# A graph network's attention layers: the destinations' term spread by products with a repeated column, and the softmax chain one group earlier

## The chip, the cores and the metric

The kernel runs on one core of one Trainium2 chip. The metric is the device time of one execution in microseconds (us); lower is better.

## The reference, cut to what matters

Two residual blocks stand behind each other: two graph-convolution layers, then five attention layers over the same 50,000 edges, sorted by destination, and 3,125 nodes. Only the attention layers are touched by the change. Each of them computes, for two heads (H = 2) of 128 features (D = 128):

```python
xw = x @ W
xj = xw[src].reshape(-1, H, D) + edge_emb.reshape(-1, H, D)
xi = xw[dst].reshape(-1, H, D)
alpha = jnp.einsum('ehd,hd->eh', xi, att_i) + jnp.einsum('ehd,hd->eh', xj, att_j)
alpha = jax.nn.leaky_relu(alpha, NEG_SLOPE)
amax = jax.ops.segment_max(alpha, dst, num_segments=N)
ea = jnp.exp(alpha - amax[dst])
denom = jax.ops.segment_sum(ea, dst, num_segments=N)
alpha = ea / (denom[dst] + EPS)
msg = xj * alpha[..., None]
aggr = jax.ops.segment_sum(msg, dst, num_segments=N)
return aggr.mean(axis=1) + b
```

Every node also has an edge to itself. The first einsum is the destinations' attention term: one number for each node and head, `x @ (W att_i)`.

## The kernel before

**Tiles.** The nodes are 25 tiles of 128 (NT = 25). The edges are 391 tiles of 128 (REAL), cut into 15 chunks: thirteen of 28 tiles, one of 16, one of 11. A chunk is worked off in groups of four tiles (seven groups in a chunk of 28).

**Gathers.** The node rows with their source term stand in `table` in HBM. GpSimd (POOL) issues one indirect DMA for each edge tile, `ring<-table,srci`, line 502, into a ring of 60 slots. Gather t reuses the slot of tile t - 60, so from the 61st on it first waits for the semaphore `sums` of the group that held this tile. POOL is thus at most 60 tiles ahead of TensorE.

**Destinations' term.** It has to lie in `ai_rows` as one row of 3,200 numbers for each head, the same in all 128 partitions. Before, VectorE (DVE) makes it by 50 dot products per layer (line 1079, into `node_ai`), TensorE (PE) transposes them (line 774), ScalarE (ACT) copies them out, and SyncE (SP) writes them to HBM and reads them back to all partitions (line 431, two transfers of 1600 KB). From `ai_rows` ACT then copies for each edge tile a window of 24 columns for both heads to `ai_win` (line 567, `windows(layer, c)`, 28 copies for a chunk), whose start it loads into a register.

**Old rows.** TensorE also transposes the 25 tiles of the layer's input (line 765, `old_tile`), and ACT copies each out of PSUM (line 587), for the products with W of the self edges (`self_tile`, line 782).

**Softmax chain.** For every chunk there is a chain of small steps between DVE, TensorE and ACT, with four names on DVE and TensorE alike: `chain_alpha` (add the gathered source term, leaky relu, transpose), `chain_scan` on DVE (running maxima), `chain_rows` (maxima across the tiles), `chain_cols` (final maxima and differences) followed by ACT's exponentials (`exps`, lines 573 and 575), and `chain_probs` (transpose back, write `est`). The chain of chunk c + 1 is woven into the groups of chunk c: `chain_alpha` stands at group number `lag(c)`, the next steps at the two groups behind it, `chain_probs` behind the last group. Group by group, DVE makes `pw` (`weigh`, line 1165), TensorE forms the sums (`aggregate`, lines 750 and 752), and DVE adds them to `acc` (`add_group`, line 1201).

**Order on ACT at a layer's start.** The copies of the old rows, then `windows(layer, 0)`, `windows(layer, 1)`, and only then `exps(layer, 0)`. `windows(layer, 1)` waits until DVE has used the windows of chunk 0.

**Order around it.** There is no scheduler: all queues are written out by hand, and semaphores tie them.

## Time and profile before

| what | value |
|---|---|
| time, median of 3 runs | 4135.25 us (4131.62 to 4136.99) |
| the profiled execution, its own time | 4165.07 us |
| its span in the profile | 4163.3 us |
| mean granted TensorE clock | 0.57 of full speed |
| busy: PE, DVE, ACT, POOL | 65%, 47%, 17%, 52% |
| DMA, mean over the span | 51 GB/s |

The profile shows one execution. A busy share is an average over the convolution part (the first 500 us) and five attention layers of some 720 to 750 us each. No engine is near 100%; what counts is which wait ends last, and that is read from the waits and from the order of time, not from the shares. "remote" and "issue" as releasers mean that the profile names no instruction that the engine waited for.

### The profile page before, as it was taken

The page shows a single profiled execution, that of the slowest core. Times are in us where ns is not written, and L with a number is a line of the kernel's source. Part 1 is how long each engine was busy: PE and PEld are TensorE (multiplying, and loading weights), DVE is VectorE, ACT ScalarE, POOL GpSimd, SP SyncE. Part 2 cuts the span into 40 slices and gives each one's busy share as a digit, 9 for nine tenths or more (in the row PEclk, how much of TensorE's full clock was granted, in tenths as well). Part 3 has the DMA queues.
Part 4 walks back from the last instruction along what each step waited for, and adds up shares of the span by engine and source line. Part 5 has one row for each costly group of instructions (what it writes and reads, how often), then busy time and mean ns, then how long its engine had stood idle before and what let it go on. Part 6 is the DMA issues. An engine that isn't in the chain of part 4 may idle for free.

```text
span 4163.3 us, 50211 instructions
## 1 busy us (share of the span) xinstructions
PE 2692.6 (65%) x14802; PEld 2154.4 (52%) x14802; DVE 1972.1 (47%) x6923; ACT 723.6 (17%) x3237; POOL 2146.3 (52%) x2359
## 2 busy tenths in 40 slices
PE   7778426665791666669266666917666691766668
PEld 6678425554561555546155555615555460555556
DVE  9866624444452444444344444534444452444445
ACT  0077321111121111101211111121111121111111
POOL 0066366666415665650656656165656615665661
PEclk9955555555575555556555555855555585555558
DMA  3211122222102222210212222022222102222221
GB/s 113 90 46 49 51 78 50 50 48 54 38 18 78 49 48 49 53 43 11 83 47 48 47 55 46 18 80 49 49 48 54 44 19 79 49 48 48 48 46 32
DMA packets 114664, 213.66 MB, mean 51 GB/s; under 512 B 35266, under 2 KB 76518, under 8 KB 113110
## 3 DMA queue, kind: packets, MB, share of 16 engines
q0 software_dynamic: 62560, 130.25, 13.8%
q1 hardware_dynamic: 51830, 80.19, 5.9%
q8 instruction: 119, 1.95, 0.2%
q14 instruction: 155, 1.27, 0.1%
HBM read 198.50 MB, written 11.80 MB: 51 GB/s over the span
## 4 chain that ended last, share of the span: by engine, by line
PE 23%; DVE 21%; POOL 19%; issue 17%; another core or an unknown queue 12%; DVEq 2%; ACTq 2%; ACT 2%; DMA 1%; POOLq 0%; SPq 0%
POOL ring L502 19%; PE bank L750 8%; PE bank L752 4%; DVE acc L1201 4%; PE bank L758 3%; DVE prod L1079 2%; PE bank L695 2%; ACTq L567 2%; DVE ring L870 1%; DVE ai_win L1098 1%; DVE alpha L1101 1%; DVEq L1024 1%; PE bank L820 1%; DVE ai_rows L955 1%
## 5 line engine op out<-in xcount | busy, mean ns | idle before, releaser
L502 POOL DMA_INDIRECT ring<-table,srci x1955 | 1877.1, 960 | 1225.5 <-issue 533.3
L750 PE MATMUL bank<-pw,ring 128*128 128x48 f32 x3910 | 1205.6, 406 | 110.3 <-DMA ring<-table,srci 61.0
L1201 DVE TENSOR_TENSOR acc<-acc,bank 128x72 f32 x1955 | 449.9, 230 | 1398.3 <-remote 745.9
L750 PEld LDWEIGHTS bank<-pw,ring 128*128 128x128 f32 x3910 | 950.0, 297 | 265.2 <-issue 132.6
L567 ACT COPY ai_win<-ai_rows 128x48 f32 x1955 | 349.5, 229 | 1496.5 <-issue 1165.6
L752 PE MATMUL bank<-onehot,est 128*36 128x24 f32 x3910 | 601.5, 240 | 0.0
L752 PEld LDWEIGHTS bank<-onehot,est 128*36 128x36 f32 x3910 | 369.3, 144 | 168.3
L708 PE MATMUL bank<-identf,alpha 128*56 128x128 f32 (+2 forms) x75 | 29.1, 388 | 472.9 <-DVE alpha L1117 259.6
L509 POOL TENSOR_TENSOR S<-S 128x128 f32<-128x128 f32 x125 | 57.2, 458 | 466.1 <-ACT S L579 461.6
L708 PEld LDWEIGHTS bank<-identf,alpha 128*56 128x56 f32 (+2 forms) x75 | 8.9, 119 | 484.8 <-issue 261.8
L484 POOL TENSOR_TENSOR ring<-ring,acc 128x512 f32<-128x512 f32 x98 | 115.2, 1177 | 277.6 <-ACT ring L532 273.8
L1098 DVE TENSOR_TENSOR ai_win<-ai_win,onehot 128x1344 f32<-128x1344 f32 (+2 forms) x75 | 109.2, 1456 | 276.9 <-issue 231.3
L758 PE MATMUL bank<-onehot,identf 128*128 128x504 f32 x310 | 208.9, 787 | 0.0
L721 PE MATMUL bank<-ones,cin 1*56 1x1 f32 (+1 forms) x300 | 37.2, 224 | 252.6 <-DVE cin L1148 161.4
L695 PE MATMUL bank<-onehot,ring 128*128 128x24 f32 x784 | 172.4, 387 | 38.8 <-DVE acc L1050 30.1
L695 PEld LDWEIGHTS bank<-onehot,ring 128*128 128x128 f32 x784 | 169.5, 331 | 40.5 <-issue 28.3
L573 ACT ACTIVATE phi<-phi 1x2 f32<-1x2 f32 x75 | 15.2, 203 | 941.0 <-issue 587.3
L734 PE MATMUL bank<-identf,bwd 56*128 56x56 f32 (+2 forms) x75 | 25.5, 340 | 227.4 <-ACT bwd L575 193.7
L721 PEld LDWEIGHTS bank<-ones,cin 1*56 1x56 f32 (+1 forms) x300 | 30.8, 185 | 273.4 <-DVE cin L1148 168.4
L1165 DVE TENSOR_TENSOR pw<-onehot,est 128x192 f32<-128x192 f32 x490 | 166.8, 353 | 0.5 <-issue 0.5
L782 PE MATMUL bank<-Wl,S 128*128 128x256 f32 x250 | 152.8, 715 | 0.0
L734 PEld LDWEIGHTS bank<-identf,bwd 56*128 56x128 f32 (+2 forms) x75 | 13.1, 175 | 250.7 <-ACT bwd L575 212.9
(205 smaller groups left out, 3278.1 us busy)
## 6 DMA issues: line engine op xcount, KB each, us to landing
ring<-table,srci POOLq DMA_INDIRECT x1955
ai_rows<-lo_dram SPq DMA_DIRECT2D x28, 896.0 KB, 4.3
ai_rows<-ai_dram SPq DMA_DIRECT2D x10, 1600.0 KB
at<-in_attr SPq DMA_DIRECT2D x65, 224.0 KB
table<-ring SPq DMA_DIRECT2D x25, 325.0 KB, 3.4
x_mid<-ring SPq DMA_DIRECT2D x1, 1600.0 KB, 7.0
result<-ring SPq DMA_DIRECT2D x24, 64.0 KB
vrow<-v_dram SPq DMA_DIRECT2D x20, 64.0 KB
```

The costliest lines, as they stand in the source:

```text
L484: GP.tensor_tensor(z, z, b1s.unsqueeze(1).broadcast_to((P, GRP, D)), ALU.add).then_inc(pre_add, 1)
L502: nc.gpsimd.indirect_dma_start(out=ring[:, slot(t), :], out_offset=None, in_=table, in_offset=bass.IndirectOffsetOnAxis(ap=srci[:, t:t + 1 ...
L567: ins = nc.scalar.copy(ai_win[:, t - TC[c] + k, :, :], ai_rows[:, :, bass.ds(base[k], WIN)])
L695: ins = nc.tensor.matmul(grp_sum(g, k)[:, 0:WIN], rows[:, g % 3, k, :], onehot[:, t, :], start=True, stop=True)
L750: nc.tensor.matmul(o[:, 0:H * WIN], ring[:, slot(t), 0:D], pw[:, g % 3, k, :, :].rearrange("p h w -> p (h w)"), start=True, stop=True)
L752: ins = nc.tensor.matmul(o[0:EC, H * WIN:REG * WIN], est[:, c % 2, t - TC[c], :], onehot[:, t, :], start=True, stop=True)
L758: nc.tensor.matmul(bank[3][:, 0:21 * WIN], identf[:, :], onehot[:, 0:21, :].rearrange("p t w -> p (t w)"), start=True, stop=True)
L782: nc.tensor.matmul(bank[3][:, 0:H * D], S[:, j, D:2 * D], Wl[:, layer % 2, :], start=True, stop=True).then_inc(s_ps, 1)
L1079: V.tensor_tensor_reduce(out=dump[:, d % NDUMP, :], in0=xt[:, j, 0:D], in1=vrow[:, 2 * h + i, :], scale=1.0, scalar=v17[:, layer, h, FA:FA ...
L1098: link(V.tensor_tensor(win, win, onehot[:, ts, :].unsqueeze(2).broadcast_to((P, k, H, WIN)), ALU.mult))
L1165: V.tensor_tensor(pw[:, g % 3, 0:n, :, :], onehot[:, t:t + n, :].unsqueeze(2).broadcast_to((P, n, H, WIN)), est[:, c % 2, k:k + n, HF:HF + ...
L1201: V.tensor_tensor(win, win, grp_sum(g, k).rearrange("p (r w) -> p r w", r=REG), ALU.add)\
```

## The change

- The destinations' term: TensorE multiplies the transposed old rows by a weight block whose 128 columns are all the same vector W att_i (`V4[...].broadcast_to((P, P))`). Each product gives the term of 512 nodes in all 128 partitions at once, so `ai_rows` is filled by copies out of PSUM: head 0 by ACT, head 1 by DVE, seven each. The 50 dots, the transpose, the write to HBM and the two broadcast reads go.
- The old rows are transposed four at a time into one PSUM bank and copied out by seven ACT copies of 512 columns instead of 25 of 128.
- For the self edges the term comes out of `self_tile`, whose product gets two more columns; DVE copies them to `node_ai` for each of the 25 tiles.
- `lag(c)` is the number of groups less 4 instead of less 3: the four chain steps move one group earlier, on DVE and on TensorE.

```diff
-DOTS = 2 * H * NT
+DOTS = H * NT
+TQ = 4
+NQ = -(-NT // TQ)
 def lag(c):
-    return max(0, len(GC[c]) - 3)
+    return max(0, len(GC[c]) - 4)
...
             for layer in range(LAYERS):
                 table_tiles(layer)
-                sp.wait_ge(aiT_sb, layer + 1)
-                sp.dma_start(ai_dram, aiT).then_inc(aiT_w, 16)
-                sp.wait_ge(aiT_w, 16 * (layer + 1))
-                for h in range(H):
-                    sp.dma_start(ai_rows[:, h, :], ai_flat[:, h * NP:(h + 1) * NP].broadcast_to((P, NP)))\
-                        .then_inc(ai_in, 16)
...
+        def ai_copy(copy, engine, layer, q, h):
+            a, b = q * TQ * P, min(NP, (q + 1) * TQ * P)
+            engine.wait_ge(ai_ps, H * NQ * layer + H * q + h + 1)
+            copy(ai_rows[:, h, a:b], bank[4 + h][:, 0:b - a]).then_inc(ai_sb[h], 1)
...
-                for j in range(NT):
-                    act.wait_ge(tr_ps, n + j + 1)
-                    nc.scalar.copy(S[:, j, D:2 * D], bank[6 + j % 2][:, 0:P]).then_inc(tr_sb, 1)
-                    if j == 1:
-                        act.wait_ge(aiT_ps, layer + 1)
-                        nc.scalar.copy(aiT, bank[3][0:H * NT, 0:P]).then_inc(aiT_sb, 1)
-                act.wait_ge(ai_in, 16 * H * (layer + 1))
+                def old_rows(q):
+                    j0, j1 = q * TQ, min(NT, q * TQ + TQ)
+                    act.wait_ge(tr_ps, n + j1)
+                    nc.scalar.copy(S[:, j0:j1, D:2 * D],
+                                   bank[6 + q % 2][:, 0:(j1 - j0) * P].rearrange("p (j n) -> p j n", n=P)).then_inc(tr_sb, 1)
+
+                for q in range(NQ):
+                    old_rows(q)
+                    if q:
+                        ai_copy(nc.scalar.copy, act, layer, q - 1, 0)
+                ai_copy(nc.scalar.copy, act, layer, NQ - 1, 0)
+                for h in range(H):
+                    act.wait_ge(ai_sb[h], NQ * (layer + 1))
                 windows(layer, 0)
                 windows(layer, 1)
                 exps(layer, 0)
...
+            def ai_product(layer, q):
+                j0, j1 = q * TQ, min(NT, q * TQ + TQ)
+                pe.wait_ge(tr_sb, NQ * layer + q + 1)
+                for h in range(H):
+                    if q:
+                        pe.wait_ge(ai_sb[h], NQ * layer + q)
+                    nc.tensor.matmul(bank[4 + h][:, 0:(j1 - j0) * P].rearrange("p (j n) -> p j n", n=P),
+                                     V4[:, layer, 2 * h:2 * h + 1].broadcast_to((P, P)), S[:, j0:j1, D:2 * D],
+                                     start=True, stop=True).then_inc(ai_ps, 1)
...
-                for j in range(NT):
-                    for h in range(H):
-                        dot(layer, j, h, 0, node_ai[:, h, j:j + 1])
...
                 def self_rows(j):
                     v.wait_ge(s_ps, n + j + 1)
+                    V.tensor_copy(node_ai[:, :, j], bank[3][:, H * D:H * D + H])
                     V.tensor_tensor(S[:, j, :], bank[3][:, 0:H * D], ebl[:, :], ALU.add)\
                         .then_inc(s_sb, 1)

+                for q in range(NQ):
+                    ai_copy(V.tensor_copy, v, layer, q, 1)
```

The first place is TensorE's queue at the start of the second attention layer, behind the last products of the layer before. L765 are the transposes of the old rows, L774 that of the dots, L708 is `chain_alpha` of chunk 0; the words in brackets are the semaphores waited for. Before:

```order
L765 MATMUL bank<-identf,ring 128x128 [waits h_sb,lay_w]
L765 MATMUL bank<-identf,ring 128x128 [waits h_sb]
L774 MATMUL bank<-identf,node_ai 50x128 [waits dotted]
L765 MATMUL bank<-identf,ring 128x128 [waits tr_sb,h_sb] x23
L708 MATMUL bank<-identf,alpha 56x128 [waits al_ready,tr_sb,aiT_sb]
```

Now (L772 the transposes, L780 the products with the repeated column):

```order
L772 MATMUL bank<-identf,ring 128x128 [waits h_sb] x8
L780 MATMUL bank<-S,V 128x512 [waits tr_sb]
L780 MATMUL bank<-S,V 128x512
L772 MATMUL bank<-identf,ring 128x128 [waits h_sb,tr_sb]
L772 MATMUL bank<-identf,ring 128x128 [waits h_sb] x3
L780 MATMUL bank<-S,V 128x512 [waits ai_sb0,tr_sb]
L780 MATMUL bank<-S,V 128x512 [waits ai_sb1]
```

Nothing waits for `dotted` any more, and each pair of products stands behind four transposes and waits for a copy of ACT and for the two copies of the pair before.

The second place is TensorE's queue at the end of a chunk of 28 tiles, between its last group and the first group of the next chunk. L721, L725 and L727 are `chain_cols`, L734 and L735 `chain_probs`. Before, behind the last group:

```order
L752 MATMUL bank<-onehot,est 36x24
L721 MATMUL bank<-ones,cin 56x1 [waits scan2]
L721 MATMUL bank<-ones,cin 56x1
L725 MATMUL bank<-phi,ones 128x2 [waits exp_phi]
L727 MATMUL bank<-phi,sel 128x1 x2
L734 MATMUL bank<-identf,bwd 128x56 [waits exp_al]
L735 MATMUL bank<-identf,fwd 128x56
L750 MATMUL bank<-pw,ring 128x48 [waits gath1,est_ready,added,issued,p_ready]
```

Now (the same steps are L725, L729, L731, L738 and L739, a group is L754 and L756):

```order
L725 MATMUL bank<-ones,cin 56x1 [waits scan2]
L725 MATMUL bank<-ones,cin 56x1
L729 MATMUL bank<-phi,ones 128x2 [waits exp_phi]
L731 MATMUL bank<-phi,sel 128x1 x2
L754 MATMUL bank<-pw,ring 128x48 [waits added,p_ready]
```

`chain_cols` has moved ahead of the last group; behind that group only `chain_probs` is left.

## Rows read from the trace of the kernel before

**Rows 1.** The page, costliest groups: the gathers (busy, mean ns, idle before).

```profile
L502 POOL DMA_INDIRECT ring<-table,srci x1955 | 1877.1, 960 | 1225.5 <-issue 533.3
```

**Rows 2.** Instructions of line 502: what POOL waited for (us, times).

```profile
  PE bank L752: 358.1, 78
  remote: 285.6, 124
```

**Rows 3.** Order of time, POOL: first gather, second and fourth attention layer (start, us).

```profile
1252.18 0.98 POOL L502 DMA_INDIRECT ring<-table,srci  x1 [5.21 <-DMA table<-ring]
...
2720.94 0.96 POOL L502 DMA_INDIRECT ring<-table,srci  x1 [5.51 <-DMA table<-ring]
```

**Rows 4.** Order of time, POOL: the 61st gather of each of the five layers.

```profile
607.94 0.94 POOL L502 DMA_INDIRECT ring<-table,srci  x1 [17.46 <-PE bank L752]
1348.45 0.94 POOL L502 DMA_INDIRECT ring<-table,srci  x1 [21.54 <-PE bank L752]
2094.80 0.94 POOL L502 DMA_INDIRECT ring<-table,srci  x1 [19.25 <-PE bank L752]
2814.84 0.94 POOL L502 DMA_INDIRECT ring<-table,srci  x1 [17.49 <-PE bank L752]
3540.53 0.94 POOL L502 DMA_INDIRECT ring<-table,srci  x1 [21.03 <-PE bank L752]
```

**Rows 5.** Order of time, ACT: first window copies, second and fourth attention layer.

```profile
1296.37 1.48 ACT L567 COPY ai_win<-ai_rows 128x48 f32 x8 [0.21 <-issue]
...
2744.31 1.77 ACT L567 COPY ai_win<-ai_rows 128x48 f32 x10 [0.21 <-issue]
```

**Rows 6.** Order of time, ACT: later window copies of the same two layers.

```profile
1317.59 0.23 ACT L567 COPY ai_win<-ai_rows 128x48 f32 x1 [2.57 <-issue]
1318.99 0.23 ACT L567 COPY ai_win<-ai_rows 128x48 f32 x1 [1.17 <-issue]
...
1336.94 4.13 ACT L567 COPY ai_win<-ai_rows 128x48 f32 x24 [0.20 <-issue]
...
2805.51 1.95 ACT L567 COPY ai_win<-ai_rows 128x48 f32 x11 [0.47 <-issue]
```

**Rows 7.** Order of time, second attention layer: ACT's last relu, TensorE, the broadcasts.

```profile
1247.58 0.31 ACT L610 ACTIVATE ring<-y 128x128 f32<-128x128 f32 x1 [0.75 <-DVE y L1298]
...
1259.61 0.41 PE L774 MATMUL bank<-identf,node_ai 128*50 128x128 f32 x1 [15.46 <-DVE node_ai L1079]
...
1261.74 0.81 SPq L431 DMA_DIRECT2D ai_rows<-ai_dram  x2
```

**Rows 8.** Order of time, all engines, from one chunk's last group through the next chunk.

```profile
1427.43 1.32 DVE L1201 TENSOR_TENSOR acc<-acc,bank 128x72 f32 x4 [0.46 <-remote]
1427.57 0.94 POOL L502 DMA_INDIRECT ring<-table,srci  x1 [2.77 <-remote]
...
1430.04 0.28 DVE L1160 TENSOR_TENSOR bwd<-bank,fwd 56x128 f32<-56x128 f32 x1
...
1431.22 0.22 DVE L1174 COPY est<-bank 128x56 f32<-128x56 f32 x1 [0.90 <-PE bank L735]
...
1432.47 0.62 DVE L1165 TENSOR_TENSOR pw<-onehot,est 128x192 f32<-128x192 f32 x2
...
1432.88 0.66 PE L750 MATMUL bank<-pw,ring 128*128 128x48 f32 x2 [1.70 <-DMA ring<-table,srci]
...
1436.58 0.94 POOL L502 DMA_INDIRECT ring<-table,srci  x1 [4.32 <-PE bank L752]
...
1456.49 0.41 PE L708 MATMUL bank<-identf,alpha 128*56 128x128 f32 x1 [5.04 <-issue]
...
1480.82 0.94 POOL L502 DMA_INDIRECT ring<-table,srci  x1 [4.32 <-PE bank L752]
```

**Rows 9.** Groups of instructions by form, PE: 504-column filler products, old-row transposes.

```profile
L758 PE MATMUL bank<-onehot,identf 128*128 128x504 f32 x310 | 208.9, 787 | 0.0
...
L765 PE MATMUL bank<-identf,ring 128*128 128x128 f32 x125 | 44.5, 427 | 78.0 <-issue 53.5 <-ACT S L587 14.0 <-ACT ring L554 10.4
```

More of the change, by code:

```diff
@@ L138, in program @@
         biasl = sb("biasl", [P, D])
-        vrow = sb("vrow", [P, 4, D])
+        vrow = sb("vrow", [P, H, D])
         V4 = sb("V4", [P, LAYERS, 4])
@@ L339, in program @@
         dotted = sem("dotted")
-        aiT_ps = sem("aiT_ps")
-        aiT_sb = sem("aiT_sb")
-        aiT_w = sem("aiT_w")
-        ai_in = sem("ai_in")
+        aj_read = sem("aj_read")
+        ai_ps = sem("ai_ps")
+        ai_sb = [sem(f"ai_sb{h}") for h in range(H)]
+        wv_sb = sem("wv_sb")
         tr_ps = sem("tr_ps")
@@ L391, in node_weights @@
             def node_weights(layer):
-                sp.dma_start(Wl[:, layer % 2, :], weights[layer * P:(layer + 1) * P, :]).then_inc(lay_w, 16)
+                sp.dma_start(Wl[:, layer % 2, 0:H * D], weights[layer * P:(layer + 1) * P, :]).then_inc(lay_w, 16)
                 sp.dma_start(ebl[:, :], edge_b[layer:layer + 1, :].broadcast_to((P, H * D))).then_inc(lay_w, 16)
                 sp.dma_start(biasl[:, :], biases[layer:layer + 1, :].broadcast_to((P, D))).then_inc(lay_w, 16)
-                for q in range(4):
-                    sp.dma_start(vrow[:, q, :], v_dram[4 * layer + q:4 * layer + q + 1, :].broadcast_to((P, D)))\
-                        .then_inc(lay_w, 16)
+                for h in range(H):
+                    q = 4 * layer + 2 * h + 1
+                    sp.dma_start(vrow[:, h, :], v_dram[q:q + 1, :].broadcast_to((P, D))).then_inc(lay_w, 16)
             def edge_weights(layer):
@@ L947, in _, with weight_columns @@
             v.sem_inc(V4_sb, 1)
+            def weight_columns(layer):
+                V.tensor_copy(Wl[:, layer % 2, H * D:H * D + H], V4[:, layer, 0:4:2]).then_inc(wv_sb, 1)
+            weight_columns(0)
             def pick(n, out):
@@ L1069, in _, with dot @@
             v.sem_inc(ln_coef, 1)
-            v.wait_ge(lay_w, 16 * 7)
+            v.wait_ge(lay_w, 16 * 5)
             dots = [0]
-            def dot(layer, j, h, i, out_col):
+            def dot(layer, j, h, out_col):
                 d = dots[0]
@@ L1078, in dot @@
                     v.wait_ge(dotted, d - NDUMP + 1)
-                V.tensor_tensor_reduce(out=dump[:, d % NDUMP, :], in0=xt[:, j, 0:D], in1=vrow[:, 2 * h + i, :], scale=1.0,
-                                              scalar=v17[:, layer, h, FA:FA + 1] if i else 0.0,
+                V.tensor_tensor_reduce(out=dump[:, d % NDUMP, :], in0=xt[:, j, 0:D], in1=vrow[:, h, :], scale=1.0,
+                                              scalar=v17[:, layer, h, FA:FA + 1],
                                               op0=ALU.mult, op1=ALU.add, accum_out=out_col).then_inc(dotted, 1)
@@ L1209, in _ @@
                 link(V.tensor_copy(node_aj[:, :, :], xt[:, :, D:ROW].rearrange("p j h -> p h j")))
-                for j in range(NT):
-                    for h in range(H):
-                        dot(layer, j, h, 0, node_ai[:, h, j:j + 1])
+                v.sem_inc(aj_read, 1)
                 link(V.tensor_tensor(ebl[:, :].rearrange("p (h f) -> p h f", h=H),
@@ L1252, in _ @@
                     if c == 10:
+                        if not final:
+                            weight_columns(layer + 1)
                         v.wait_ge(lay_e, 32 * (layer + 1))
@@ L1284, in _ @@
                 else:
-                    v.wait_ge(lay_w, 16 * 7 * (layer + 2))
+                    v.wait_ge(lay_w, 16 * 5 * (layer + 2))
                 for j in range(NT):
```

51 lines of the change are left out of this document (26 added, 25 removed).

## The prediction, made blind

> **What bounds the kernel now.** I read the costliest groups first, then what the gathers waited for, then the order of time at a layer's start and inside a layer. The gathers are the largest group, 1,877 us busy, yet POOL is idle for 1,225 us before them [rows 1]. Of that, 533 us are the 0.30 us between two gathers [rows 1]; 358 us are waits for TensorE's group sums and 286 us waits with no named releaser [rows 2], which in the order of time also fall on gathers that need a group's sums. So inside a layer POOL runs as far ahead as the ring of 60 slots lets it, then stands until a group is summed: a layer goes at the pace at which the first sums of each chunk come out, not at POOL's own 1.25 us for a gather.
>
> Two places hold these waits. The first is the 61st gather of each layer: stalls of 17.46, 21.54, 19.25, 17.49 and 21.03 us, 97 us together [rows 4]. The reader is to see that chunk 0 has not given its first sums when the ring is full. The second repeats at each chunk boundary: 4.32 us at 1436.58 [rows 8]. It comes again at 1480.82, 44.2 us later, as 4.32 us. There are eleven boundaries per layer, 55 in all, from the 89th gather to the 369th; most show about 4.3 us.
>
> **The start of a layer.** In the second attention layer ACT is free at 1247.9 [rows 7]. TensorE then waits 15.46 us for the dots, transposes them at 1259.61, the broadcasts go out at 1261.74, and ACT's first window copy starts at 1296.37 [rows 5, 7], 44.2 us after the first gather [rows 3]. What held it was not the broadcast alone: the 25 old-row copies stand ahead of it on ACT.
>
> Now the change. Dots, transpose, write and broadcasts go. TensorE can do two batches of transposes before ACT is free, then alternates: two products and four transposes per round. A 512-column product is not in the trace; the nearest is the filler of 504 columns, 208.9 us for 155 products (each shows as two rows), 1.35 us at the mix of clocks there; a transpose costs 44.5/125 = 0.36 us [rows 9]. A round is 2 x 1.35 + 4 x 0.36 = 4.1 us. Six rounds from 1248.5, a short seventh and the last copy end near 1274, 22 us after the first gather. ACT's and DVE's copies lie beside the products. So the windows start 22 us earlier than before in this layer.
>
> What is that worth? The trace has the answer without the change, because layers differ. In the fourth layer the windows already started 23.4 us after the first gather, in the second 44.2 us [rows 3, 5]. Yet the stalls are 17.49 and 21.54 us [rows 4]: 20.8 us earlier bought 4.05 us. The reason is ACT's pace. While POOL gathers, a window copy starts every 1.40 us and every fourth takes 2.80, 7.0 us for four; after POOL has stopped, 24 copies take 4.13 us [rows 6]. In the fourth layer the quick pace came back only at 2805.51 [rows 6], some 8 us after the gathers had stopped (2814.84 - 17.49 = 2797.4 [rows 4]). Chunk 0's exponentials stand behind the windows of chunk 1 on ACT, 56 copies in all, so at 7.0 us for four they cannot be through before the ring is full. What ends last is this return of the quick pace, and that hangs on POOL. With 0.195 us of stall per us of window start, 22 us gives 17.2 us of stall in each layer: 0.3 + 4.3 + 2.0 + 0.3 + 3.8 = **11 us** saved over five layers. The lower bound is 0; the upper one the whole 97 us [rows 4], if the slow pace does not come.
>
> At full TensorE clock the rounds would be shorter and the windows start up to 10 us earlier; by the same slope this is 2 us per layer at most. The Trainium skill (TensorE: Matmul & The Clock Gate, Part 1: The HAM clock gate) says that TensorE keeps its full clock of 2.4 GHz only while it is kept busy, and the products would keep it busier here. Its effect stays within those 2 us.
>
> The first gather itself waits for the table write [rows 3], whose dots stay. It does not move.
>
> **The chain one group earlier.** Take the boundary in rows 8. POOL gets the slots of the last group at 1427.57, issues four gathers (5.0 us) and stands 4.32 us until the next chunk's first group is summed, 9.01 us after 1427.57. In these 9 us DVE adds the last group (1427.43 to 1428.75), only then does the columns step (to 1430.32), ACT the exponential, TensorE the transposes, DVE `est` (1431.22) and `pw` (1432.47), TensorE the group (1432.88), POOL goes on at 1436.58. With the new order the columns step stands before the last group is added, and its exponential runs beside that addition. Then from 1428.75: `est` 1.25 us (1431.22 to 1432.47), 0.41 us to the group, 3.70 us to POOL: 1434.1 instead of 1436.58, **2.4 us** per boundary. The stall shrinks from 4.32 to 1.9, so it is not used up and all of 2.4 us would be on the path: 55 x 2.4 = 132 us.
>
> I don't take all of it. TensorE stands 5.04 us before `chain_alpha` [rows 8], and its fifth group was already through by then. Now it stands before the rows step for the scan instead, which DVE ends about 1 us later, and the sixth group follows. POOL's other stalls (2.8 us before 1427.57) release what the sums of the middle groups hold up, and a shorter stall at the boundary may lengthen them. Bounds: 0 and 2.4 us. I take two thirds, 1.6 us, since the chain in rows 8 is a strict sequence that the new order really shortens: 55 x 1.6 = **88 us**.
>
> **What it adds.** One more filler product per layer in the twelfth chunk, 1.35 us [rows 9], so 5 x 1.35 = 7 us if nothing hides it; I take 4. The 25 copies of two columns to `node_ai` in each layer lie in DVE's idle time (47% busy over the span); uncovered, at about the 0.2 us of a small copy (`est`, 0.22 us [rows 8]), 25 us in all. The seven pairs of products and their copies are in the 22 us above. Two vrow loads less and the moved wait for weights cost nothing: the loads go out in mid-layer.
>
> **Sum.** -11 - 88 + 4 = -95 us. The profiled execution took 4165.07 us (its span 4163.3), so one of after should show about 4070. It stands 30 us over the median of the runs, and I take the saving off both alike: 4135.25 - 95 = 4040 us.
>
> **The rivals.**
> - *Likeliest (0.45)*: both terms as above, 1.0 to 2.4 us per boundary: 3995 to 4085, 4040 in the middle.
> - *The chain gives nothing (0.22)*. POOL's stalls may be needed by the rest: ACT's pace of 7.0 us for four copies ends only when POOL stands [rows 6], and DVE sees sums late while POOL runs ("remote", 286 us [rows 2]). Then a shorter stall at the boundary comes back as a longer one two groups on, and the 9 us of stall in a chunk stay. For it: the waits without a releaser. Against: in rows 8 each step follows its cause within 0.5 us. Time: 4135 - 11 + 4 = 4128, to 4110 with a little of the chain's gain.
> - *The slow pace does not come at a layer's start (0.15)*. The 3.2 MB of broadcasts fall just where ACT turns slow. If they are its cause, 56 copies take some 10 us, chunk 0 is summed before the ring is full, and the 97 us of rows 4 go whole: 4135 - 97 = 4038 without the chain's gain, 3950 with it. Against: the slow pace lasts until POOL stops, long after the transfers. The Trainium skill (Runtime: NRT & Kernel Launch, Instruction fetch mechanics) says that an engine's instructions are fetched ahead and the fetch is mostly hidden; by it the 1.40 us per copy are not a lack of instructions, and ACT would do its windows at the quick pace once whatever loads the core is gone.
> - *Slower (0.10)*. TensorE's sixth group now stands behind the rows step and so behind DVE's scan. POOL needs its sums for the last four gathers of the chunk after next. If they come so late that POOL stands once more per chunk, a stall like the 2.77 us in rows 8 is added at each boundary and eats the 2.4: from +0 to 55 x 2.77 = 152 us, 4135 to 4287, I say 4175. It decides when the sixth group's sums come over 1.9 us later than now.
> - *No change to be told (0.08)*: the small terms cancel, 4127 to 4143. Under 0.2% (8.3 us) a measurement of this kernel can't be told from no change.
>
> **How the numbers follow.** The time is that of the likeliest, 4040. The range 3960 to 4127 takes the likeliest (0.45), nearly all of the second case (0.21) and most of the third (0.13), 0.79 together; the likeliest alone is 3995 to 4085. Faster: 0.45 + 0.21 + 0.15 = 0.81; within 0.2%: 0.08 and what the second case leaves, 0.09; slower: 0.10.
>
> **What the profile of after would show.** Right: window copies start 12 to 25 us after the first gather in every layer; the 61st gather's stall is near 17 us in all five; the boundary stall falls from 4.3 to about 2 us, and the distance of two boundary stalls from 44 to 42 or 42.5 us. Wrong, in order: a 61st gather without a stall (third case); boundary stalls shorter but 44 us apart (second); a new stall per chunk before the sixth group's slots (fourth). The weakest step is the two thirds of 2.4 us.

## The result, and the profile after

| | kernel before | changed kernel |
|---|---|---|
| median of the runs, us | 4136.12 (4 runs, 4131.62 to 4146.59) | 3939.68 (4 runs, 3930.15 to 3949.26) |
| ratio | | 0.9522, 95% interval 0.9488 to 0.9555 |
| profiled execution, us (its span) | 4165.07 (4163.3) | 3949.26 (3947.2) |

The change saves 196 us. The forecast was 95, and 3940 lies below its range (3960 to 4127). The direction was right and the size was half of it.

The table holds for one kind of chip. The experiments ran on five numbered chips, and these fall into two kinds: on two of them (9 and 4) the kernel before takes 4135 and 4132 us, as here, and on three (6, 11 and 12) it takes 3445 to 3448 us. On the one of these three where the changed kernel itself was run (6) it is 0.8% *slower*. I come to that below. "The first kind" are the chips at 4135 us, "the second kind" those at 3445.

Where the time went can be read from one group. These are the gathers of the changed kernel on the page (columns as in [rows 1]; its line 495 is line 502 of before):

```profile
L495 POOL DMA_INDIRECT ring<-table,srci x1955 | 1891.2, 967 | 1023.2 <-issue 536.8 <-remote 299.8 <-PE bank L756 139.3
```

The pauses between two gathers ("issue") and the gathers themselves are what they were [rows 1]. The two waits for group sums were 358.1 and 285.6 us [rows 2], together 643.7; now they are 139.3 and 299.8, together 439.1. That is 205 us less. Gathers and pauses took 18 us more. The two spans differ by 216 us; the 29 us that are left lie behind the last gathers of the layers. There the first two layers take 40 us less, for in before TensorE had a low clock in just these two (below), and the other three 12 us more.

The first place, the start of a layer. Order of time of the changed kernel, POOL, the 61st gather of each of the five layers, as in [rows 4]:

```profile
599.09 0.94 POOL L495 DMA_INDIRECT ring<-table,srci  x1 [10.39 <-PE bank L756]
...
1282.25 0.94 POOL L495 DMA_INDIRECT ring<-table,srci  x1 [12.60 <-PE bank L756]
...
1974.95 0.94 POOL L495 DMA_INDIRECT ring<-table,srci  x1 [16.52 <-PE bank L756]
...
2660.27 0.95 POOL L495 DMA_INDIRECT ring<-table,srci  x1 [16.49 <-PE bank L756]
...
3351.04 0.94 POOL L495 DMA_INDIRECT ring<-table,srci  x1 [16.50 <-PE bank L756]
```

Together 72.5 us instead of 96.8 [rows 4]: 24 us less, where 11 were forecast. TensorE and ACT in the second attention layer, in order of time: the products that spread the term, and the window copies that answer to [rows 5, 6]:

```profile
1195.86 1.88 PE L780 MATMUL bank<-S,V 128*128 128x512 f32 x4
1197.58 0.60 PE L772 MATMUL bank<-identf,ring 128*128 128x128 f32 x4
1198.02 1.88 PE L780 MATMUL bank<-S,V 128*128 128x512 f32 x4
```

```profile
1206.06 2.23 ACT L565 COPY ai_win<-ai_rows 128x48 f32 x12 [1.47 <-issue]
...
1217.91 0.23 ACT L565 COPY ai_win<-ai_rows 128x48 f32 x1 [1.87 <-issue]
1219.31 0.23 ACT L565 COPY ai_win<-ai_rows 128x48 f32 x1 [1.17 <-issue]
...
1251.51 0.23 ACT L565 COPY ai_win<-ai_rows 128x48 f32 x1 [2.57 <-issue]
1252.91 0.23 ACT L565 COPY ai_win<-ai_rows 128x48 f32 x1 [1.17 <-issue]
1254.31 0.23 ACT L565 COPY ai_win<-ai_rows 128x48 f32 x1 [1.17 <-issue]
1255.71 0.23 ACT L565 COPY ai_win<-ai_rows 128x48 f32 x1 [1.17 <-issue]
```

A round of two products and four transposes takes 2.16 us (1195.86 to 1198.02) and not 4.1, since TensorE had its 2.4 GHz here (granted clock 1.00 from 1195 to 1199 us). The windows start 12.6 us after the layer's first gather (at 1193.4), not 22; over the five layers it is 10.0 to 16.1 us. Then ACT falls into the slow pace of [rows 6] all the same: 1.40 us for a copy and 2.80 for every fourth. The first 12 copies still go at the quick pace, though POOL has been gathering for 12.6 us by then; I come back to that at the end. No broadcast runs any more. So the third rival, that the broadcasts cause the slow pace, is refuted.

The second place, the chunk boundary. Order of time of the changed kernel over one boundary, all engines, as in [rows 8]:

```profile
1477.46 0.15 DVE L1176 COPY carry_col<-bank 56x2 f32<-56x2 f32 x1 [1.75 <-remote]
...
1479.16 0.31 ACT L573 ACTIVATE bwd<-bwd 56x128 f32<-56x128 f32 x1 [9.19 <-issue]
1479.52 0.35 PE L738 MATMUL bank<-identf,bwd 56*128 56x56 f32 x1 [2.86 <-issue]
...
1481.27 1.31 DVE L1221 TENSOR_TENSOR acc<-acc,bank 128x72 f32 x4 [2.14 <-remote]
1481.40 0.94 POOL L495 DMA_INDIRECT ring<-table,srci  x1 [2.58 <-remote]
1482.50 0.21 DVE L1194 COPY est<-bank 128x56 f32<-128x56 f32 x1
...
1483.74 0.62 DVE L1185 TENSOR_TENSOR pw<-onehot,est 128x192 f32<-128x192 f32 x2
...
1484.15 0.66 PE L754 MATMUL bank<-pw,ring 128*128 128x48 f32 x2 [4.17 <-DVE pw L1185]
...
1487.85 0.94 POOL L495 DMA_INDIRECT ring<-table,srci  x1 [1.47 <-PE bank L756]
```

The columns step, the exponential and its transposes are through before the last group is added, and `est` follows the addition at once. From the slots of the last group to POOL's next start it is 6.45 us (1481.40 to 1487.85) where it was 9.01. The stall is 1.47 us instead of 4.32. The boundary before this one in the same trace is at 1446.42 and the next at 1529.17, so they lie 41.4 us apart, where it was 44.2. This boundary is a fair sample: in POOL's order of time the 55 stalls at the boundaries are 235.6 us before and 92.5 now (4.28 and 1.68 us each), and the mean distance of two boundaries goes from 44.0 to 41.1 us. All other waits behind the 88th gathers of the layers go from 285.8 to 251.5 us together.

### The profile page after: what moved, and what is told of

Read it like the earlier page. It is cut to its first block, busy times and chain, and to the rows that moved or that the text cites. A ratio compares the mean times of both kernels' runs of the same rounds, so it can differ in the third digit from the quotient of the medians.

```text
span 3947.2 us, 50027 instructions
## 1 busy us (share of the span) xinstructions
PE 2719.3 (69%) x14947; PEld 2152.7 (55%) x14947; DVE 1939.4 (49%) x6588; ACT 738.0 (19%) x3177; POOL 2160.9 (55%) x2359
## 4 chain that ended last, share of the span: by engine, by line
DVE 35%; PE 21%; another core or an unknown queue 18%; issue 13%; DVEq 5%; ACTq 4%; POOL 3%; ACT 2%; DMA 0%; POOLq 0%; SPq 0%
DVE acc L1221 9%; PE bank L754 6%; PE bank L762 4%; ACTq L565 3%; PE bank L756 3%; POOL ring L495 2%; DVE pw L1185 2%; DVEq L1044 2%; DVE ai_win L1118 2%; PE bank L699 2%; DVE alpha L1121 2%; DVEq L1221 2%; DVE ee L1120 1%; DVE prod L1099 1%
## 5 line engine op out<-in xcount | busy, mean ns | idle before, releaser
L754 PE MATMUL bank<-pw,ring 128*128 128x48 f32 x3910 | 1206.7, 406 | 247.5 <-DVE pw L1185 180.5
L754 PEld LDWEIGHTS bank<-pw,ring 128*128 128x128 f32 x3910 | 935.8, 295 | 382.3 <-DVE pw L1185 190.8
L1221 DVE TENSOR_TENSOR acc<-acc,bank 128x72 f32 x1955 | 449.9, 230 | 1247.8 <-remote 726.8
L565 ACT COPY ai_win<-ai_rows 128x48 f32 x1955 | 358.4, 229 | 1860.7 <-issue 1749.9
L756 PE MATMUL bank<-onehot,est 128*36 128x24 f32 x3910 | 600.2, 239 | 7.8 <-issue 7.8
L756 PEld LDWEIGHTS bank<-onehot,est 128*36 128x36 f32 x3910 | 368.6, 144 | 179.6 <-issue 12.6
L717 PE MATMUL bank<-identf,fwd 56*1 56x56 f32 (+1 forms) x150 | 24.3, 259 | 262.3 <-issue 132.6
L729 PE MATMUL bank<-phi,ones 1*128 1x2 f32 x150 | 41.5, 344 | 174.5 <-ACT phi L571 174.4
L797 PE MATMUL bank<-Wl,S 128*128 128x258 f32 x250 | 153.7, 716 | 0.0
L541 ACT ACTIVATE ring<-ring,acc 128x128 f32<-128x128 f32 x392 | 124.4, 388 | 56.9 <-PE bank L699 42.3
L729 PEld LDWEIGHTS bank<-phi,ones 1*128 1x128 f32 x150 | 35.0, 289 | 176.6 <-ACT phi L571 175.0
```

What stands on the lines that cost most here:

```text
L541: ins = nc.scalar.activation(rows[:, g % 3, k, :], pre[:, g % 3, k, :], ACT.Relu, scale=n_e[:, t:t + 1])
L565: ins = nc.scalar.copy(ai_win[:, t - TC[c] + k, :, :], ai_rows[:, :, bass.ds(base[k], WIN)])
L754: nc.tensor.matmul(o[:, 0:H * WIN], ring[:, slot(t), 0:D], pw[:, g % 3, k, :, :].rearrange("p h w -> p (h w)"), start=True, stop=True)
L756: ins = nc.tensor.matmul(o[0:EC, H * WIN:REG * WIN], est[:, c % 2, t - TC[c], :], onehot[:, t, :], start=True, stop=True)
L797: nc.tensor.matmul(bank[3][:, 0:H * D + H], S[:, j, D:2 * D], Wl[:, layer % 2, :], start=True, stop=True).then_inc(s_ps, 1)
L1221: V.tensor_tensor(win, win, grp_sum(g, k).rearrange("p (r w) -> p r w", r=REG), ALU.add)\
```

## The experiments

Times are medians, each beside runs of the kernel before on the same chip. Where a kernel ran on several chips, the text under the quoted expectation says which.

**The lag alone.** The kernel before with one line changed:

```
-    return max(0, len(GC[c]) - 3)
+    return max(0, len(GC[c]) - 4)
```

> The kernel of before with the chain one group earlier (lag 4 instead of 3) and nothing else of the change. Theory A (the chain behind each chunk's last group is a strict sequence, and the shift takes about 3 us out of each of the 55 chunk boundaries, whatever fills ai_rows): chunk distance 44.1 us falls to about 41.1, boundary stall 4.3 to 1.4 us, the 61st gather's stalls stay at 17 to 21 us, time about 3965 us. Theory B (the gain comes from the lighter load of the new destinations' term, and the shift by itself is eaten by longer stalls elsewhere): chunk distance stays near 44, time 4110 or more.

Measured 3969.25 us, ratio 0.9579 (0.9519 to 0.9639), and on another chip of the first kind 3973.46, ratio 0.9607 (0.957 to 0.9644), as `lag_again`. By the medians the lag makes 165 of the 196 us (159 on the other chip), 3.0 us for each of the 55 boundaries. Theory A holds: the mean distance of two boundaries is 41.1 us in the trace of lag_only, the 55 boundary stalls are 90.0 us together, 1.64 each, and the 61st gather still stalls for 17.4 to 21.4 us. From the first gather to the last, summed over the layers, before takes 3049.4 us and lag_only 2893.8. That is 156 us, so some 10 of the 165 lie behind the last gathers.

**The attention term alone.** The changed kernel with the old line back:

```
-    return max(0, len(GC[c]) - 4)
+    return max(0, len(GC[c]) - 3)
```

> The kernel of after with the chain back at its old place (lag 3). Theory A: window copies start 13 to 16 us after the first gather, the 61st gather's stalls are 10 to 16 us, chunk distance 44.1 us as before, time about 4136 - 26 = 4110 us. Theory B: most of the 196 us is kept, time 3950 to 4000.

Measured 4089.53 us, ratio 0.9851 (0.9789 to 0.9912), and 4112.93, ratio 0.9951 (0.9918 to 0.9984), on the other chip of the first kind, as `term_again`. So it is 19 to 45 us alone, and the two intervals don't meet; from lag_only to the changed kernel it is 30. Theory B, that most of the gain is kept without the lag, is refuted. One line from the page of each, the gathers:

```profile
L502 POOL DMA_INDIRECT ring<-table,srci x1955 | 1889.3, 966 | 1056.5 <-issue 535.8 <-remote 315.7 <-PE bank L752 157.7
```

```profile
L495 POOL DMA_INDIRECT ring<-table,srci x1955 | 1873.7, 958 | 1192.9 <-issue 537.9 <-PE bank L756 322.4 <-remote 285.4
```

The first is lag_only, the second term_again. The waits for sums are 473.4 and 607.8 us, where before has 643.7 [rows 2] and the changed kernel 439.1. The lag takes 170 us off, the term 36 without the lag and 34 with it: the two parts add up.

**Which step of the chain.** The changed kernel, but with the columns step behind the last group, as it was, in the chunks of 28 tiles. The alpha and rows steps stay a group earlier:

```
+def cols_at(c):
+    return 6 if len(GC[c]) == 7 else lag(c) + 2
...
-                        if more and i == lag(c) + 2:
+                        if more and i == cols_at(c):
...
-                        if more and i == q + 2:
+                        if more and i == cols_at(c):
```

> The kernel of after, but chain_cols alone is back behind the last group in chunks of 28 tiles; chain_alpha and chain_rows stay one group earlier. Theory A as the prediction priced it (what shortens the boundary is that the columns step comes before the last group's addition): chunk distance back to 43.5 to 44.1, boundary stall 4 us, time about 4080. Theory C (the earlier rows step is what counts, since its result was held back while POOL gathers): chunk distance stays under 42, time 3940 to 3970.

Measured 4039.39 us, ratio 0.9731 (0.9666 to 0.9797), between the two ranges. By the medians the columns step is worth 100 us, the alpha and rows steps about 65 of the lag's 165. The traces say it without TensorE's clock behind the last gathers (below): from the first gather to the last, summed over the layers, it is 3014.6 us with a lag of 3 (term_again), 2954.5 here and 2862.5 in the changed kernel. So, taken in this order, the alpha and rows steps are worth 60 us and the columns step 92. POOL in order of time in this kernel, three of its waits over two chunks:

```profile
2175.24 0.94 POOL L499 DMA_INDIRECT ring<-table,srci  x1 [7.72 <-PE bank L760]
...
2221.77 0.94 POOL L499 DMA_INDIRECT ring<-table,srci  x1 [1.68 <-remote]
...
2261.71 0.94 POOL L499 DMA_INDIRECT ring<-table,srci  x1 [7.78 <-PE bank L760]
```

Here one boundary costs 7.72 us and the next but one 7.78; around the one between them no wait is over 2.7 us. The two take 86.5 us together, 43.2 for a chunk, between the 44.2 of before and the 41.4 of the changed kernel; the mean over all five layers is 42.8. My theory of a strict chain (the columns step makes it all) is too simple: the other two steps gain as well.

**ACT's first exponentials ahead of the windows of chunk 1.** On the changed kernel:

```
                 windows(layer, 0)
-                windows(layer, 1)
                 exps(layer, 0)
+                windows(layer, 1)
```

> The kernel of after with ACT's exponentials of chunk 0 put ahead of the windows of chunk 1 at each layer's start. If the prediction's reason for the remaining stall at the 61st gather holds (the exponentials stand behind 28 window copies at 7.0 us for four), chunk 0 is summed about 45 us after the first gather and the 61st gather has no stall; the windows of chunk 1 then end at about 80 us, and DVE waits for them before the second group's addition, so a stall comes at the 65th gather instead: 0 to 12 us saved per layer, 3880 to 3940 in all. If something else held the exponentials, the stall at the 61st gather stays at 10 to 16 us, time 3940.

Measured 3918.63 us, ratio 0.9454 (0.9393 to 0.9514), 21 us below the changed kernel. That was against the kernel before on its own chip, so the difference rests on two ratios whose intervals overlap. The trace speaks for it. The 61st gather of the second attention layer in this kernel:

```profile
1282.96 0.94 POOL L495 DMA_INDIRECT ring<-table,srci  x1 [8.70 <-remote]
```

This wait is 7.9 to 9.0 us in every layer, 42 together, where the changed kernel has 72.5. So the slow copies of chunk 1 ahead of chunk 0's exponentials held the 61st gather for 30 of these 72.5 us. The expectation had no stall left there and a new one at the 65th gather; the 65th has none (0.3 us at most), and what holds the last 8 us of each layer stays open.

**The same, and two steps further, on a chip of the second kind.** Four kernels on one chip, of which the third and fourth are new:

> The changed kernel itself once more, as the base for the three others on the same chip: 3925 to 3950 us, ratio to before 0.950 to 0.955.

> The changed kernel with ACT's first exponentials ahead of the windows of chunk 1, once more. If they really take chunk 0 off the windows of chunk 1, the 61st gather stalls 8 us instead of 10 to 16 and the time is 15 to 35 us under that of the changed kernel in the same call; if the first difference was chance, within 8 us of it.

The third is exps_first with the last step of the chain ahead of the last group, on TensorE and DVE:

```
                     for i, g in enumerate(GC[c]):
+                        if more and len(GC[c]) >= 4 and i == len(GC[c]) - 1:
+                            chain_probs(layer, c + 1)
                         aggregate(layer, g)
...
-                        chain_probs(layer, c + 1)
+                        if len(GC[c]) < 4:
+                            chain_probs(layer, c + 1)
```

> exps_first, and in each 28-tile chunk the last step of the next chunk's chain (transposes of the exponentials, est, first two pw) ahead of the last group on TensorE and DVE. Theory A (the chain's length still sets the boundary): TensorE's wait for pw at the boundary, 4 to 6 us, goes, the boundary stall of 1.4 us goes and part of the stalls of about 2 us behind it: 1 to 2.5 us for each of 55 boundaries, 3780 to 3865 us. Theory B (the chain has been brought off the path by the change, and what is left of POOL's stalls is how late DVE and POOL see TensorE's sums while gathers run): 3895 to 3935, no change to be told.

The fourth is exps_first with `len(GC[c]) - 5`. So that DVE's sums over the windows stay spread over the first three groups, its two conditions `q < 3` and `q >= 3` become `q < 2` and `q >= 2`:

> exps_first with the chain one group earlier again (alpha behind the third group, rows behind the fourth, columns behind the fifth). The last add of a chunk and est behind it stay where they are, and the change already put the columns step ahead of them. Theory A and B both: nothing left to gain from the columns step, 3900 to 3930. A rival (each group of earlier start is worth the 3 us that the first one was): 55 x 3 less, near 3755. Another (the rows and the alpha step now delay the middle groups): 3940 to 4000.

| kernel | us | ratio to before | 95% |
|---|---|---|---|
| before | 3445.02 | | |
| changed kernel (after_again) | 3474.45 | 1.0083 | 1.0065 to 1.0102 |
| exps_again | 3470.20 | 1.0078 | 1.0059 to 1.0098 |
| probs_4 | 3539.35 | 1.0274 | 1.0253 to 1.0294 |
| lag5_exps | 3501.78 | 1.0167 | 1.0146 to 1.0188 |

None of the expectations held, for all were written for 4135 us. The kernel before takes 690 us less here, and the order of the kernels is turned round: the two further steps that were to gain lose most, and exps_first and the changed kernel can't be told apart. The gathers of the changed kernel on this chip, and its first window copies of the second attention layer, which answer to 1206.06 and what follows above:

```profile
L495 POOL DMA_INDIRECT ring<-table,srci x1955 | 1912.0, 978 | 641.9 <-issue 592.4 <-DMA table<-ring 47.6 <-PE bank L756 1.8
```

```profile
1119.66 5.11 ACT L565 COPY ai_win<-ai_rows 128x48 f32 x28 [1.47 <-DVE ai_rows L510]
1129.52 4.83 ACT L565 COPY ai_win<-ai_rows 128x48 f32 x28 [4.75 <-DVEq L1122]
```

The wait for sums is 1.8 us instead of 439.1. ACT copies 28 windows in 5 us *while POOL gathers*; on the first kind the second 28 took 43 us (1231.99 to 1274.9). There is nothing left for the lag to gain.

**The missing trace of before, and the parts, once more.**

> The kernel before, for its trace on the chip of this call. If its time is near 4135 us, ACT takes 7.0 us for four window copies while gathers run and POOL stands 110 to 120 us in each layer; if it is near 3445 us, 28 window copies take 5 us beside the gathers and POOL stands under 20 us in a layer, so that only 36 us per chunk of gathers and the tail count.

> The kernel before with the lag of 4 alone. On a chip where before takes 4135 us: 3960 to 3980, as it did. On one where it takes 3445 us, two theories of why the changed kernel is 0.8% slower there. L (the lag: chain_alpha waits for the gathers of its chunk to land one group sooner than they can, and the last chunks end later): 3465 to 3480. T (the attention term costs more than it saves, by the start of each layer): within 5 us of before.

> The changed kernel with the lag of 3. On a chip where before takes 4135 us: 4085 to 4100, as it did. On one where it takes 3445 us: by L, 3430 to 3450, no slower than before; by T, 3460 to 3480.

These three ran on a chip of the first kind: before_again took 4117.57 us, and the results of the other two stand above. So L and T were not told apart there. The next four ran on the second kind.

> The kernel before, for its trace. Near 4135 us as on two chips, or near 3445 us as on a third; in the second case POOL stands under 20 us in a layer and the tail behind the last gather is what differs from the changed kernel: under 88 us from the last gather to the next layer's first, and chunk 0's est under 45 us before that of chunk 1.

> The changed kernel, but in each layer POOL stops before its 13th gather until ACT has both first chunks' windows. On a chip where before takes 4135 us: if ACT's slow pace hangs on POOL's gathers, the quick pace (28 copies in about 5 us) comes back within 10 us of the stop, the pause ends 15 to 25 us after it began, the 61st gather no longer stalls, and the time is within 50 us of the changed kernel (3920 to 3990). If ACT's pace is slow for another reason, the 56 copies take 70 us or more: 4100 and over. On a chip where before takes 3445 us: the pause costs 10 to 17 us in each layer, 3525 to 3560.

> As before: exps_first with the last step of the chain ahead of the last group. On a chip where before takes 4135 us: A (the wait for pw at the boundary is the bound) 3780 to 3865; B (what is left is how late TensorE's sums are seen while gathers run) 3895 to 3950. On one where it takes 3445 us: 3535 to 3545, as it did.

> As before: exps_first with the chain one more group earlier. On a chip where before takes 4135 us: nothing left to gain 3900 to 3930; the rival of 3 us at each boundary once more, 3755; the rival of delayed middle groups 3940 to 4000. On one where it takes 3445 us: 3495 to 3510, as it did.

The edit of pool_pause on the changed kernel is this:

```
                 for t in range(REAL):
+                    if t == 12:
+                        pool.wait_ge(win_ready, layer * NC + 2)
```

before_third took 3432.39 us, pool_pause 3528.18 (ratio 1.0251, 1.021 to 1.0293), probs_again 3540.84 (1.0273, 1.0252 to 1.0295) and lag5_again 3500.89 (1.0159, 1.0138 to 1.0181). The last two repeat the chip before. The pause cost what was expected on this kind; on the first kind, where it would have told something, it never ran. In before_third, the gathers' group:

```profile
L502 POOL DMA_INDIRECT ring<-table,srci x1955 | 1920.3, 982 | 642.0 <-issue 592.4 <-DMA table<-ring 47.7 <-PE bank L752 1.8
```

It is that of the changed kernel to 0.1 us of waiting, and the gathers themselves take 8 us more here. So the 29 us must lie behind the last gathers of the layers: there the trace of the changed kernel takes 445.5 us in all and that of before 407.4. Order of time, POOL's last gather of the second attention layer and DVE's last additions of its sums: in before_third, then in the changed kernel (after_again), then with a lag of 5 (lag5_exps, whose own base with a lag of 4 is exps_again):

```profile
1598.64 0.94 POOL L502 DMA_INDIRECT ring<-table,srci  x1 [0.30 <-issue]
...
1630.60 0.95 DVE L1201 TENSOR_TENSOR acc<-acc,bank 128x72 f32 x3 [1.12 <-PE bank L752]
```

```profile
1608.43 0.94 POOL L495 DMA_INDIRECT ring<-table,srci  x1 [0.30 <-issue]
...
1646.38 0.95 DVE L1221 TENSOR_TENSOR acc<-acc,bank 128x72 f32 x3 [1.12 <-PE bank L756]
```

```profile
1609.24 0.94 POOL L495 DMA_INDIRECT ring<-table,srci  x1 [0.30 <-issue]
...
1657.06 0.95 DVE L1221 TENSOR_TENSOR acc<-acc,bank 128x72 f32 x3 [1.12 <-PE bank L756]
```

From the last gather to the start of the last addition: 32.0 us, then 38.0, then 47.8. Over the five layers it is 31.5 to 33.3 us, 38.0 to 41.0 (38.1 to 42.2 in exps_again) and 46.6 to 48.9. The reader is to see that each group of earlier start makes this tail longer. In probs_4, the slowest, it is 48.7 to 50.8 us.

**The lag alone on the second kind.**

> The changed kernel with POOL stopped before its 13th gather of each layer until ACT has both first chunks' windows. On a chip where before takes 4135 us: if ACT's slow pace hangs on POOL's gathers, the pause ends 15 to 30 us after it began, the 61st gather does not stall, and the time is 3920 to 3990; if not, 4100 and over. On a chip where before takes 3445 us: 3518 to 3545, as it did there (the pause was 10 to 12 us).

> exps_first with the last step of the chain ahead of the last group of each 28-tile chunk. On a chip where before takes 4135 us: A (the wait for pw is the bound) 3780 to 3865; B (what is left is how late TensorE's sums are seen while gathers run) 3895 to 3950; and C, by what the other kind of chip showed (each layer's last chunks end 10 us later), up to 50 us on top of either. On a chip where before takes 3445 us: 3535 to 3545, as it did.

> The kernel before with the lag of 4 alone. On a chip where before takes 4135 us: 3960 to 3980, as on two such chips. On one where it takes 3445 us: if the lag makes the loss of the changed kernel, 3465 to 3480 with a tail of 38 to 42 us from the last gather to the last addition; if the attention term makes it, within 5 us of before.

These ran on the second kind, too. pause_last took 3528.11 us and probs_last 3542.03, as on the chips before. lag_last took 3466.76 us, ratio 1.0054 (1.0035 to 1.0074). Its rows for the same tail:

```profile
1607.24 0.94 POOL L502 DMA_INDIRECT ring<-table,srci  x1 [0.30 <-issue]
...
1648.30 0.95 DVE L1201 TENSOR_TENSOR acc<-acc,bank 128x72 f32 x3 [1.12 <-PE bank L752]
```

41.1 us instead of 32.0 (37.8 to 43.6 over the five layers). The lag alone makes 19 of the 29 us, and the tail shows where: theory L holds, and theory T, within 5 us of before, does not. What the attention term adds to it, 0.3%, is within what the two intervals leave open.

Why does an earlier chain end later? DVE in the changed kernel on this kind, in order of time (after_again):

```profile
1356.65 0.35 DVE L1185 TENSOR_TENSOR pw<-onehot,est 128x192 f32<-128x192 f32 x1
1361.90 0.26 DVE L1131 TENSOR_TENSOR alpha<-alpha,ring 128x56 f32<-128x56 f32 x1 [4.90 <-DMA ring<-table,srci]
...
1362.77 1.31 DVE L1221 TENSOR_TENSOR acc<-acc,bank 128x72 f32 x4 [0.35 <-issue]
```

The alpha step needs all 28 gathers of its chunk. With POOL never held up, these land last of all, and DVE stands in front of that step with the remaining groups' additions queued behind it. With the lag of 4 four groups are still to be added after the step, before it was three. When POOL stops, what is still queued is the tail. It can be counted: behind the start of the last gather DVE has 31 additions left in before_third (35 in one layer), 38 or 39 in after_again, 37 to 42 in lag_last and 43 to 47 in lag5_exps. That is seven or eight per step of the lag, nearly two groups and not the one that the order alone would give; where the second comes from is open. The reading is argued from the order, this count and the tails at three lags; no run took the wait alone away.

## Why the prediction was right and wrong

**What bounds the kernel: right for this kind of chip.** POOL waited for the first sums at the two places named. Of the 205 us that the waits gave, 167 are at these two (24 at the 61st gathers, 143 at the boundaries), and 34 of the rest in the other stalls of the chunks.

**The chain one group earlier: right in mechanism, and the step that failed.** The prediction worked out 2.4 us per boundary, a stall going from 4.32 to 1.9, and then wrote "I take two thirds, 1.6 us", 88 us in all. lag_only measured 165 us, 3.0 us per boundary, and the boundary stall went to 1.47 here, 1.64 on average. So 1.6 us was mis-sized, and the undiscounted 2.4 us (132 us) was low too.

Which part of the working failed is told by cols_late. The 2.4 us price one step alone, the columns step ahead of the last addition. It brought 92 us between the gathers, 100 by the medians: 1.7 to 1.8 us per boundary, less than 2.4 and close to the 1.6 that was taken. The alpha and rows steps stand in the working only as a reason to take less; their gain is put at nothing. They brought 60 to 65 us. This is the step that failed. By what path they gain wasn't traced.

The other way to add up lag_only, by stalls: the boundary stalls fell by 146 us (235.6 to 90.0), the other waits behind the 88th gathers by 24 (285.8 to 261.8), while gathers and pauses took 15 us more. The some 10 us that are left lie outside the waits, and there the traces show one thing: TensorE's clock. In before, the 40 us behind the last gather of the first attention layer and behind that of the third read so (busy time of each engine, then TensorE's granted clock as a share of 2.4 GHz):

```profile
1120.00:1160.00 40.00, 38.53 (x130) 24.51 (x130) 16.61 (x63) 2.18 (x13) 0.00 (x0) 0.50 0.03 7
2612.00:2652.00 40.00, 39.65 (x211) 25.44 (x211) 25.07 (x95) 2.58 (x14) 0.00 (x0) 0.93 0.04 12
```

At 0.50, which is 1.2 GHz, TensorE got through 130 matmuls in the 40 us, at 0.93 through 211. The layers at the low clock take about 20 us longer from the last gather to the last addition (80.2 and 80.3 us, against 58.1 to 60.5 in the other three). They can be counted in the traces of the first kind: with a lag of 3 it was two of five layers in before, none in before_again and two in term_again (and three in term_only, whose profiled execution took 4150.83 us, 61 above its median). With a lag of 4 it was none of twenty (the changed kernel, exps_first, lag_only, lag_again), but two of five in cols_late, which has that lag and the columns step late. So a part of the lag's gain, up to 20 us for each layer so spared, seems to be the clock and not the boundary; one trace for each kernel can't say how often. It would also account for the profiled execution of before, which stood 30 us above its median, as the prediction noted and left without a cause: before_again, without such a layer, took 4117.57 us.

The reason for the discount was that the other stalls of a chunk might grow. They did not: between two boundaries the changed kernel has 2.42 and 2.58 us, where before had waits of the same size beside its 4.32, and over all chunks they fell, as the sums above show. And the second rival, that POOL's stalls are needed and the chain gives nothing, is refuted by lag_only alone.

**The start of a layer: a term of 11 us that measured 24 at the 61st gather and 30 in time.** Two numbers of the working failed. The windows began 10 to 16 us after the first gather instead of 22, for the products ran at 2.4 GHz. The prediction had priced this at "2 us per layer at most" by its slope of 0.195. But the slope, drawn from two layers of before, does not hold that far down: the first two layers went from 17.46 and 21.54 us of stall to 10.39 and 12.60, 16 us together, and the other three, with the slow pace in full, to 16.5 each. Half of the 16.5 us is due to the slow copies of chunk 1 ahead of chunk 0's exponentials, as exps_first shows by putting them behind: 7.9 to 8.5 in these three layers.

The Trainium skill (TensorE: Matmul & The Clock Gate, Part 1: The HAM clock gate) was cited for the full clock while TensorE is kept busy; the trace agrees for this stretch, where TensorE was busy throughout from 1195 to 1199 us at a granted clock of 1.00 and a round took 2.16 us, against the 4.1 that was worked out at the mix of clocks. The first of the two rows above goes the other way: TensorE was busy for 38.53 of 40 us and had 0.50.

**What it adds: +4 us**, not to be seen on its own. The filler product belongs to the lag, so lag_only has it as well. It may be what keeps the clock up in the tail; that was not tried apart.

**The slower rival** (0.10): it did not come on the first kind. On the second kind the kernel is slower, but by another mechanism than the one described: not the sixth group's sums, but the wait for the gathers to land in front of the alpha step, which then makes the tail longer. No case of the prediction had it.

**What the range missed.** 3940 is the likeliest case with both terms larger than it had them: the chain at 3.0 us per boundary where at most 2.4 were allowed, and the start at 30 us where 11 were taken. That the range came within 20 us of it is owed to the third case, whose mechanism didn't come. With the undiscounted 2.4 and the measured start the sum would have been 4135 - 132 - 30 + 4 = 3977, inside the range; of the last 37 us the traces show 11 more at the boundaries (143 for 132) and 34 in the other stalls, which were counted as a risk, less the 18 us that gathers and pauses took more; the 10 that are left lie outside, where the clock is.

## What to carry to other kernels

When several steps of a chain move together, price each of them, with either sign, and not only the one that the trace shows last: here the unpriced ones made over a third of what the lag gained. Keep the doubt for the range, and there let the terms be high together. When a wait is removed on one engine, look whether the bound that takes its place is a stall (then the rest of the chain is still worth shortening) or the engine's own pace (then an earlier step only moves a wait in front of other work, and the tail pays). And before a change is kept, look at it on more than one chip: this one saves 4.8% on one kind and loses 0.8% on the other.

## What the runs showed that was not expected

- **Two kinds of chips.** Same program, same instruction count, same bytes, 4135 us on one kind and 3445 on the other. The 733 us between the spans of before (4163.3 and 3430.6) are 642 us of waits for sums, less 102 us of longer gathers and pauses, plus 193 us between the last gather of a layer and the first of the next (or the end). Each numbered chip was measured at one time only, so it isn't shown that the chip makes the difference and not something else that held at that time.
- **On the first kind ACT turns slow while POOL gathers**, 7.0 us for four copies of 0.23 us. In before and in the changed kernel it does so only after the first 10 to 16 copies of a layer, however long POOL has been gathering by then (10 to 44 us). So the gathers alone don't make the slow pace; it looks like something of which ACT has a store at first, but no run tests that. DVE's waits for additions have a part that names no releaser ("remote": 726.8 us in the changed kernel); half of the 158 additions so marked start over 2.1 us after TensorE's last product for the sums has ended, where it is 0.14 us for those that wait for TensorE by name. On the second kind neither exists. DVE's additions in both, from the groups of instructions:

```profile
L1221 DVE TENSOR_TENSOR acc<-acc,bank 128x72 f32 x1955 | 449.9, 230 | 1247.8 <-remote 726.8 <-PE bank L756 208.8 <-issue 87.7
```

```profile
L1221 DVE TENSOR_TENSOR acc<-acc,bank 128x72 f32 x1955 | 449.5, 230 | 775.8 <-PE bank L756 509.1 <-DVE alpha L1123 35.8 <-issue 27.2
```

  The instructions take the same time (230 ns); what differs is what stands between them. What in the chip makes it stays open. The run that would have shown whether POOL's gathers are the cause (pool_pause) never ran on the first kind, and the bound that is left there after the change (probs_4 and lag5_exps) was not measured either.
- **exps_first has the lowest median on the first kind** (3918.63 us). On the second kind the kernel before stays the fastest of all that were run.
